# Upper halves of two layer norms made from the rows in front of the norm, in a fused transformer kernel

## The reference, cut to what matters

```
x = x + tanh(g_xattn[0]) * attention(layernorm(x), ctx)           # 8 heads, rotary, 128 context rows
x = x + tanh(g_ffn[0])   * ternary_ffn(layernorm(x))              # 512 -> 2048, relu^2, -> 512, low-rank part
x = x + tanh(g_xattn[1]) * (layernorm(x) @ W1.T + mean(ctx) @ W2.T + b)
x = x + tanh(g_ffn[1])   * bit_ffn(layernorm(x))                  # int8 activations, ternary weights, gelu

layernorm(x) = (x - mean(x)) / sqrt(var(x) + 1e-5)
```

## Time and profile before

| what | value |
|---|---|
| time, three runs | 1179.39, 1174.64, 1177.76 us; median 1177.76 |
| profiled execution, span | 1176.7 us (the page lists no other time for it) |
| TensorE busy | 1094.3 us, 93% |
| VectorE busy | 953.5 us, 81% |
| ScalarE busy | 799.4 us, 68% |
| GpSimd busy | 591.5 us, 50% |
| mean granted TensorE clock | 0.978 of full speed |

### The profile page before, as it was taken

How to read it: one execution, slowest core, us unless ns; L and a number is a source line. 1 busy time by engine, 2 the same in 40 slices (tenths; PEclk the granted TensorE clock), 3 DMA queues, 4 the chain that set the end, 5 groups by cost and what they waited for, 6 DMA issues and landing times.

```text
span 1176.7 us, 22172 instructions
## 1 busy us (share of the span) xinstructions
PE 1094.3 (93%) x8270; PEld 677.4 (58%) x8558; DVE 953.5 (81%) x1989; ACT 799.4 (68%) x1575; POOL 591.5 (50%) x567
## 2 busy tenths in 40 slices
PE   5776699999999999999899999999999999999997
PEld 5544456474655656475655656475656656564654
DVE  4796868778789888788878798898879886998667
ACT  3988947676683958576584857676674957586545
POOL 4243545464653746454544656555545555564431
PEclk9888799999999999999999999999999999999999
DMA  9959651434525343533625252443436242432210
GB/s 339 367 153 309 204 122 47 99 81 77 126 59 117 69 116 73 104 81 68 126 53 136 57 123 68 89 110 77 108 55 145 45 119 61 103 69 55 68 45 27
DMA packets 273802, 128.11 MB, mean 109 GB/s; under 512 B 247568, under 2 KB 248080, under 8 KB 272016
## 3 DMA queue, kind: packets, MB, share of 16 engines
q1 hardware_dynamic: 273136, 125.73, 41.8%
q10 hardware_dynamic: 560, 0.96, 0.3%
HBM read 57.19 MB, written 8.39 MB: 56 GB/s over the span
## 4 chain that ended last, share of the span: by engine, by line
PE 55%; ACT 17%; DVE 16%; POOL 5%; issue 4%; DMA 2%; SPq 0%; ACTq 0%; DVEq 0%
PE ps L1861 14%; PE ps L1835 10%; PE ps L1904 6%; PE ps L1920 5%; PE ps L1788 5%; ACT e L966 4%; PE ps L1735 4%; PE ps L1883 4%; ACT rl L1002 3%; ACT hid L1007 2%; ACT sq L1013 2%; PE ps L1760 1%; DVE st L1369 1%; PE ps L1841 1%; PE ps L1775 1%
## 5 line engine op out<-in xcount | busy, mean ns | idle before, releaser
L1835 PE MATMUL ps<-xT,fcT 128*128 128x256 f16 x2048 | 262.5, 276 | 10.8 <-ACT rl L1002 7.1
L749 POOL TENSOR_TENSOR rs<-ve,nhalf 128x1 f32<-128x1 f32 x160 | 101.7, 638 | 306.1 <-DVE ve L1374 222.8
L1861 PE MATMUL ps<-pjT,hid 128*128 128x512 fp8e4 x1024 | 232.3, 379 | 2.6 <-POOL hid L776 1.6
L1835 PEld LDWEIGHTS ps<-xT,fcT 128*128 128x128 fp8e4 x2048 | 200.1, 99 | 52.6 <-ACT rl L1002 10.0
L776 POOL TENSOR_TENSOR hid<-sq,hid 128x512 f16<-128x512 f32 x128 | 163.1, 1279 | 80.3 <-ACT sq L1013 79.4
L1861 PEld LDWEIGHTS ps<-pjT,hid 128*128 128x128 f16 x1024 | 98.0, 98 | 98.3
L1002 ACT ACTIVATE rl<-ps,rsf 128x256 f32<-128x256 f32 x256 | 106.4, 469 | 25.0 <-PE ps L1841 24.8
L966 ACT ACTIVATE e<-ps,nmb,sig 128x128 f32<-128x128 f32 x256 | 113.1, 462 | 7.2 <-DVE nmb L1412 6.9
L1904 PE MATMUL ps<-w1T,q4T 128*128 128x512 fp8e4 x480 | 114.2, 379 | 0.7 <-issue 0.6
L1058 ACT ACTIVATE q<-h 128x2048 f16<-128x2048 f32 x30 | 57.3, 1910 | 79.3 <-DVE h L1531 79.3
L781 POOL TENSOR_TENSOR e<-e,einv 128x512 f32<-128x512 f32 x64 | 70.1, 1100 | 78.5 <-DVE einv L1416 78.5
(11 more groups left out here) (243 smaller groups left out, 2025.7 us busy)
## 6 DMA issues: line engine op xcount, KB each, us to landing
xb<-in_x SPq DMA_DIRECT2D x16, 512.0 KB, 3.6
xa<-in_x SPq DMA_DIRECT2D x15, 512.0 KB, 4.0
out<-r SPq DMA_DIRECT2D x30, 256.0 KB, 2.3
rope<-in_rope SPq DMA_DIRECT2D x16, 384.0 KB, 3.2
h<-in_w1T SPq DMA_DIRECT2D x6, 1024.0 KB, 5.8
h<-in_w2T SPq DMA_DIRECT2D x6, 1024.0 KB, 6.4
h<-in_wkvT SPq DMA_DIRECT2D x2, 1024.0 KB, 12.6
hid<-in_w_fc SPq DMA_DIRECT2D x2, 1024.0 KB, 9.9
```

The lines of the kernel that those rows point to most:

```text
L1835: pe.matmul(ps[:, FFN0 + m % 2, a * G:(a + 1) * G], fcT[:, k, f * P:(f + 1) * P], xT2[:, xs, k, :], start=(xs == 0 and k == 0), stop=False)
L1861: mm = pe.matmul(ps[:, FFN0 + t, :], hid[:, xs, c, t * P:(t + 1) * P], pjT[:, c, :], start=(c == 0 and xs == 0), stop=(c == FC - 1 and xs ...
```

## The change

ScalarE no longer copies the normed rows. It computes the upper half itself from the rows in front of the norm, as rows * rs + shift, with rs and shift as columns (one number per row). VectorE makes the shift = -mean * rs, a new 128x1 operation (ln_shift), directly in front of ln_apply. The normed rows are still made by VectorE, for the lower half. The waits change with it: ScalarE waits for the shift instead of the normed rows; GpSimd's lower halves wait for both the upper half and the normed rows; add_cb, which overwrites r2, waits for the upper half as well. Two semaphores of the setup (c_rsf, c_sc) are folded into others, which makes room for the new ones. The tables of the order are the same.

```diff
+        shift = sb("shift", [P, 2, TILES], F32)
...
             def x2_lo(g, t):
                 need(pool, x2hi, TILES, g, t)
+                need(pool, xn2_done, TILES, g, t)
                 rest(x16f[:, t, 1, :], xn2[:, t, :], x16f[:, t, 0, :], x2lo)
...
                 need(pool, x3hi, TILES, g, t)
+                need(pool, xn3, TILES, g, t)
                 rest(x16b[:, t, 1, :], x3n_of(g)[:, t, :], x16b[:, t, 0, :], x3lo)
...
                 need(pool, xn3, TILES, g, t)
+                if not final(g):
+                    need(pool, x3hi, TILES, g, t)
                 pool.tensor_tensor(r2_of(g)[:, t, :], r2_of(g)[:, t, :], cb[:, g // PER_BATCH, :], ALU.add).then_inc(x2c, 1)
...
             def x2_hi(g, t):
                 need_dma(act, xT2_in[t], g - 1)
-                need(act, xn2_done, TILES, g, t)
-                act.activation(x16f[:, t, 0, :], xn2[:, t, :], ACT.Copy).then_inc(x2hi, 1)
+                need(act, shift2, TILES, g, t)
+                act.activation(x16f[:, t, 0, :], r1[:, g % 2, t, :], ACT.Identity, bias=shift[:, 0, t:t + 1],
+                               scale=rs[:, 1, t:t + 1]).then_inc(x2hi, 1)
...
                 need_dma(act, q4T_in[t], g - 1)
-                need(act, xn3, TILES, g, t)
-                act.activation(x16b[:, t, 0, :], x3n_of(g)[:, t, :], ACT.Copy).then_inc(x3hi, 1)
+                need(act, shift3, TILES, g, t)
+                act.activation(x16b[:, t, 0, :], r2_of(g)[:, t, :], ACT.Identity, bias=shift[:, 1, t:t + 1],
+                               scale=rs[:, 2, t:t + 1]).then_inc(x3hi, 1)
...
+            def ln_shift(rsem, done, g, n, t):
+                need(dve, rsem, TILES, g, t)
+                dve.tensor_scalar(shift[:, n - 1, t:t + 1], mv[:, n, t, 0:1], rs[:, n, t:t + 1], -1.0, ALU.mult, ALU.mult)\
+                    .then_inc(done, 1)
...
             def ln2_apply(g, t):
+                ln_shift(rs2, shift2, g, 1, t)
                 if t == 0:
                     need(dve, sq_done, FC // 2, g - 1, FC // 2 - 1)
                 ln_apply(rs2, xn2_done, g, 1, t, r1[:, g % 2, t, :], xn2[:, t, :])
...
             def ln3_apply(g, t):
+                if not final(g):
+                    ln_shift(rs3, shift3, g, 2, t)
                 ln_apply(rs3, xn3, g, 2, t, r2_of(g)[:, t, :], x3n_of(g)[:, t, :])
```

More of the change, by code:

```diff
@@ L259, in build @@
          c_vhi, c_vlo, c_cs, c_csb, c_cps, c_cb, c_tanh, c_wchain, c_scale, c_b2, c_rows, c_thr, c_rowd, c_quant, c_quantg,
-         c_tern, c_quantp, c_lowps, c_low, c_lowzero, c_lowF, c_lowt, c_lowact, c_bnd, c_rsf, c_scd,
-         c_scps, c_sc, c_asum, c_asumps, c_mean, c_round, c_lift, c_clip) = [sem(n) for n in (
+         c_tern, c_quantp, c_lowps, c_low, c_lowzero, c_lowF, c_lowt, c_lowact, c_bnd, c_scd,
+         c_scps, c_asum, c_asumps, c_mean, c_round, c_lift, c_clip) = [sem(n) for n in (
             "d_ctx d_wv d_kr d_wq d_wo d_wx d_wc d_small d_rows d_u d_b1 c_const c_kps c_vps c_kru c_krot "
@@ L264, in build @@
             "c_vhi c_vlo c_cs c_csb c_cps c_cb c_tanh c_wchain c_scale c_b2 c_rows c_thr c_rowd c_quant c_quantg c_tern c_quantp "
-            "c_lowps c_low c_lowzero c_lowF c_lowt c_lowact c_bnd c_rsf c_scd c_scps c_sc c_asum "
+            "c_lowps c_low c_lowzero c_lowF c_lowt c_lowact c_bnd c_scd c_scps c_asum "
             "c_asumps c_mean c_round c_lift c_clip").split()]
@@ L279, in build @@
         (ln1, rs1, xn1, x1hi, x1lo, q_ps, rot_mul, rot_sum, q_hi, q_lo, s_ps, s_max, s_bias, s_exp, s_inv,
-         s_norm, p_hi, p_lo, pv_ps, ao_hi, ao_lo, wo_ps, x1_done, ln2, rs2, xn2_done, x2hi, x2lo, low_ps,
+         s_norm, p_hi, p_lo, pv_ps, ao_hi, ao_lo, wo_ps, x1_done, ln2, rs2, shift2, xn2_done, x2hi, x2lo, low_ps,
          part_ps, part_b, low_b, low_r, low_done) = [sem(n) for n in (
              "ln1 rs1 xn1 x1hi x1lo q_ps rot_mul rot_sum q_hi q_lo s_ps s_max s_bias s_exp s_inv "
-             "s_norm p_hi p_lo pv_ps ao_hi ao_lo wo_ps x1_done ln2 rs2 xn2_done x2hi x2lo low_ps "
+             "s_norm p_hi p_lo pv_ps ao_hi ao_lo wo_ps x1_done ln2 rs2 shift2 xn2_done x2hi x2lo low_ps "
              "part_ps part_b low_b low_r low_done").split()]
@@ L287, in build @@
             "up_ps relu sq_done hid_hi hid_lo down_ps down_mul x2_done").split()]
-        (ln3, rs3, xn3, x3hi, x3lo, x2c, wx_ps, x3_done, ln4, rs4, z4, q4_done, x3b, w1_ps,
+        (ln3, rs3, shift3, xn3, x3hi, x3lo, x2c, wx_ps, x3_done, ln4, rs4, z4, q4_done, x3b, w1_ps,
          h_done, gelu, sqsum, z5, rs5, q5_round, q5_done, w2_ps, out_done) = [sem(n) for n in (
-             "ln3 rs3 xn3 x3hi x3lo x2c wx_ps x3_done ln4 rs4 z4 q4_done x3b w1_ps "
+             "ln3 rs3 shift3 xn3 x3hi x3lo x2c wx_ps x3_done ln4 rs4 z4 q4_done x3b w1_ps "
              "h_done gelu sqsum z5 rs5 q5_round q5_done w2_ps out_done").split()]
@@ L996, in up_act @@
                 if first(g) and m == 0:
-                    act.wait_ge(c_rsf, 1)
+                    act.wait_ge(c_bnd, 7)
                     for place in (0, 1):
@@ L1245, in hidden_scale @@
                 dve.wait_ge(c_bnd, 6)
-                dve.tensor_scalar(rsf[:, :], scf[:, :], rho[:, :], None, ALU.mult).then_inc(c_rsf, 1)
+                dve.tensor_scalar(rsf[:, :], scf[:, :], rho[:, :], None, ALU.mult).then_inc(c_bnd, 1)
             def mix_row():
@@ L1352, in prepare @@
                     dve.wait_ge(d_rows, 32)
-                    dve.tensor_scalar(scbc[:, :], ps[:, 0, :], c1[:, :], None, ALU.mult).then_inc(c_sc, 1)
+                    dve.tensor_scalar(scbc[:, :], ps[:, 0, :], c1[:, :], None, ALU.mult).then_inc(c_scd, 1)
                     dve.tensor_scalar(b2bc[:, :], b2bc[:, :], tg[:, 3:4], None, ALU.mult).then_inc(c_b2, 1)
@@ L1456, in x2_out @@
                 if first(g) and t == 0:
-                    dve.wait_ge(c_sc, 1)
+                    dve.wait_ge(c_scd, 3)
                 need(dve, down_ps, TILES, g, t)
@@ L1815, in up @@
                     pe.wait_ge(c_quantp, 16)
-                    pe.wait_ge(c_sc, 1)
+                    pe.wait_ge(c_scd, 3)
                 if m == 0:
```

## The result

The changed kernel takes 1188.65 us in the median of four runs (1187.17 to 1193.33), the kernel before 1178.58 us in the runs beside it. The two medians are 10.1 us apart; the ratio on record, which isn't that of the medians, is 1.0108 with a 95% interval of 1.0087 to 1.013: slower by 12.7 us of 1177, at least by 10. The forecast was 1185.2 us and 7.4 us of loss. One later run of the kernel before took 1911 us at a mean clock of 0.56; it is left out of the ratios.

A forecast was written before the change was run, and what follows sets the result against it. TensorE, busy 97% of the steady stretch, was taken as the bound, its short waits leading to other engines. Terms 3.0 + 2.5 + 2.1 - 0.2 + 0 = 7.4 us gave 1185.2 us against the runs' median, range 1175 to 1197.

The forecast's parts named there:

- the main step: GpSimd's addition after the third norm must wait for ScalarE's upper half, about 24 us later in all, which delays TensorE.
- the term of the wait: Cost to TensorE of GpSimd's late additions: 3.0 us at three followed places plus 2.5 us for the rest.
- the three places: Late additions at 1077.96, 572.98 and 768.11 us, followed to TensorE: 1.3, 0.9 and 0.8 us lost.
- The remaining places: The other 16.1 us of later additions on GpSimd, put at 2.5 us, with ends of 0.8 and 6.1.
- most are short and have gaps behind them: Reason given for pricing the other 16.1 us of GpSimd's new waits at only 2.5 us.
- VectorE's 2.1 us: 62 new 128x1 shifts at 214 ns, 13.3 us of work, of which the chain's 16% counts: 2.1 us.
- The upper end of 13.3 us: Highest cost of VectorE's 62 shifts, if all their work counted; the other end was 0.
- ScalarE at 0: 62 longer activations add 11.5 us of work, but 36 end earlier and 26 later; put at 0.
- Second norm -0.2: Its upper half ends 0.15 us earlier where ScalarE waited: a gain of 0.2 us, ends 0 and -1.0.
- Same by cover: Rival: the late additions are covered because much of TensorE's input was ready before; 1180 us, chance 0.24.
- Faster by ScalarE's earlier start: Rival: ScalarE's upper halves start earlier and shorten TensorE's waits, down to 1171 us; chance 0.12.
- Much slower by collisions: Rival: late GpSimd additions meet VectorE work and stretch it, 14 us in all, 1192 us; chance 0.18.

The follow-up runs named there:

- e4: Kernel before with only the added wait of GpSimd's addition for ScalarE's upper half of the third norm: 1189.64 us, ratio 1.0093.
- e3: Changed kernel with GpSimd's addition writing to the second norm's dead input rows, so without the wait for ScalarE: 1180.27 us, ratio 1.0022.
- e1: Changed kernel with the second norm put back as before, only the third norm changed: 1187.75 us, ratio 1.0089.
- e6: e3 with the addition's wait for ScalarE put back for tile 1 of each group, 15 of 30 additions: 1185.02 us, ratio 1.0079.
- e5: e3 with the addition's wait for ScalarE put back for tile 0 of each group, 15 of 30 additions: 1185.28 us, ratio 1.0075.
- e8: Kernel before with the 62 VectorE shifts added but read by nobody, and the setup's two semaphores folded: 1179.97 us, ratio 1.0034.
- e7: e3 with the second norm put back as before, leaving 30 shifts and 30 longer activations: 1176.59 us, ratio 1.0009.
- e2: Changed kernel with the third norm and the addition's wait put back as before, only the second norm changed: 1182.08 us, ratio 1.0033.
- e10: e9 with the third norm changed as well, its upper half made from the rows in front of the norm: 1184.79 us, ratio 1.0067.
- e9: Kernel before with GpSimd's addition writing to other rows and not waiting for the third norm, except in the last group: 1184.45 us, ratio 1.0068.
- e12: Changed kernel with rotation sums put in front of the second tile's addition on GpSimd in the fifth and tenth group: 1191.38 us, ratio 1.0126.
- e11: Kernel before with ScalarE's 62 upper halves in the longer two-column form; the new column also moved buffers by 32 bytes: 1184.41 us, ratio 1.0074.

## Why the prediction came out as it did

**Right: the main step.** The added wait of GpSimd's addition is the cause. It alone costs 10.9 us (e4, 8.0 to 13.8), and taking it away gives back 10.1 (the changed kernel's +12.7 less e3's +2.6; 8.4 by their medians). Its marks came as written: idle time before the addition over 45 us (59.8), released by ScalarE; scores over 7.5 us (10.7); mix of the 15th group over 1.5 us (2.02); TensorE's idle time after 180 us up by more than 4 us (10.1).

**Mis-sized: the term of the wait.** 3.0 + 2.5 = 5.5 us were put there, 8 to 11 were measured. Of the three places two were right: 1.1 us near 1088 for 1.3, 0.7 near 580 for 0.9. The third, 768 us, was put at 0.8 and cost 3.1: the first 1.6 as the upper end of the prediction had it (0 to 1.5), the rest by a fall of TensorE's clock, which no term had and which e1, e4 and e6 don't have at this place, after waits of 2.02 to 2.22 us (they lose 1.4 to 1.6 us there). The remaining places were put at 2.5 us, 16% of 16.1; they lost 4.5 (9.4 less these three). The additions came about as late as computed (22.5 to 26 us for 24), so the size that failed is the price of a late one, and the step is "most are short and have gaps behind them": e5 and e6 show that 15 waits of either tile are enough for 6 to 7 us, so the loss isn't the affair of a few places. Whether the two halves simply add up isn't shown: they stand 6.2 + 6.7 = 12.9 us above e3, for 10.1 with both, a difference that the intervals, 1.4 to 2.6 us to either side, cover.

**The other terms.** VectorE's 2.1 us: e8 has 4.0 (2.6 to 5.5), which lies above it, and e7 with half of the shifts and of the longer activations 1.1 (-0.2 to 2.4), which agrees with it; the place isn't known. The upper end of 13.3 us was no end: a shift takes up 0.12 us of VectorE's queue and not 0.21, 7.8 us in all. ScalarE at 0: no run shows it alone, e7 holds it under 2.4 us for 30 of the 62. The 0.15 us by which an upper half ends earlier came out: at 21 of the third norm's 30 tiles it ends 0.27 us earlier behind the norm's start, which the shift puts 0.12 us later. Second norm -0.2: the sign was wrong, e2 has +3.9, of which its 32 shifts are a part that no run separates; its trace shows 2.1 us at one transfer (last section), which no row of before shows. That the whole came out 3.5 us above the forecast's 1185.2 and inside its range is in part the width of the range: the main term alone was short by 3 to 5 us.

**The rivals.** "Same by cover" fails by e4. "Faster by ScalarE's earlier start" fails by e2, and by e7 and e10, which are not under their counterparts; a gain of a microsecond that the shifts take back isn't excluded. "Much slower by collisions": VectorE's busy time rose by 5.6 us, far from the 14 that were its mark. But the mechanism exists: the longest of the third norm's rows goes from 1.38 to 1.59 us, and e9, which brings GpSimd's addition beside the norm on purpose, stretches it by 6.4 us in all. Here the Trainium skill, "SBUF — State Buffer", section "SBUF: two separate sides", holds that a VectorE instruction in a mode that uses two ports, or with two inputs in SBUF, and a GpSimd instruction exclude each other, and that the second one waits for the other's whole instruction. The trace agrees for the norm's 128x512, in e9 (1.48 us for 0.54, ending 0.28 us behind the addition) as in the kernel before (1.38 us, ending 0.28 us behind a lower half on GpSimd); in which mode it runs no row says. The prediction left the condition out when it asked whether a shift would wait as well. It didn't: seven of the 62 shifts start while GpSimd is in the middle of a 128x512 instruction, and they take 203 to 208 ns.

No kernel here beats the one before. e7 comes nearest, with no difference that can be measured.

## What to carry to other kernels

When a reader of a buffer moves to another engine, look first at who overwrites the buffer: the new wait lands on the writer's queue and is paid by everything behind it, here with some 10 us for additions that start 0.5 us later in the median of 30 tiles. Give the writer another buffer (rows that are dead by then cost no memory) rather than a wait. And don't take idle time in front of an instruction for slack to be removed: in an order written out by hand it may be what keeps two engines off each other; test it by taking the wait away, not by arguing. And before a place in the trace is given a price, look at the clock of both executions: a fall in one of them is as large as many a step.

## What the runs showed of the hardware

**A fall of the clock at a short wait.** From 178 to 1155 us, where TensorE is otherwise at 1.00, the 14 kernels' executions have 15 falls to 0.50, of 3.4 us each. Each stands at a wait of TensorE of 1.94 to 3.06 us, mostly behind it (780 us, rows above), in two cases from within it. Such a fall costs up to 1.7 us on top of the wait: 1.5 us at 780 us, 1.6 at 1091 us in e5. The length of the wait doesn't tell whether it comes: 17 other waits of 1.91 to 2.89 us had none, among them 2.89 us at 588 us in e1 and 2.02 us at 1098.63 us in the changed kernel. At 182 us, behind a wait of 2.2 us, the clock fell in the changed kernel and in e3, where the step is 3.3 and 3.4 us, and not in e2, e5, e6 and e12, where it is 2.1 or 2.2. What decides is open.

**Two packets behind an instruction packet.** In the changed kernel, e2, e3, e5, e6 and e12, which all have the second norm changed, the same transfer (second group, second tile, issued near 180 us) lands 4.2 to 4.4 us after its issue; in the kernel before and e1, e4, e7 to e10, which have not, 2.7 or 2.8 (3.0 in e11). Queues in the changed kernel, packets, MB and share, for the microseconds from 180 and from 181:

```profile
q8 instruction: 1, 0.02, 6.3%
q1 hardware_dynamic: 42, 0.01, 3.8%
...
q1 hardware_dynamic: 2, 0.00, 0.3%
```

All but two of the transfer's packets are through when one packet of 0.02 MB of instructions is moved, and the last two follow a microsecond later. TensorE waits for it with no releaser named:

```profile
177.86 1.23 SPq L651 DMA_TRANSPOSE xT<-x16f  x1
...
182.18 0.40 PE L1816 MATMUL ps<-xT,vcol 128*32 128x256 f16 x8 [2.17 <-issue]
```

All 14 traces have such an instruction packet of 16 KB here, of 0.9 to 1.7 us, and its place in time goes with the delay. In the six kernels with the delay it starts 0.04 to 0.17 us before the last of the transfer's other packets, and the two late ones, of 4 bytes each, come within 0.02 us of its end. In the eight without, it starts 0.03 us before the transfer's last packet at the earliest, and up to 0.5 us behind it. That it holds the two back fits all 14, and no run moved it alone; what ties its place to the second norm's change isn't known.

**Thirty-two bytes.** Buffers moved by 32 bytes, off the multiples of 64, made most turning transfers 0.3 to 0.6 us longer (e11, rows above) and raised the transfer queue's share of the engines from 35.8 to 39.8% between 180 and 1176 us. One direction of one move was tried. The Trainium skill, "DMA: Bandwidth & Descriptors", section "DMA Transpose (X-bar)", asks for 32-byte alignment in SBUF; both programs keep it, and the transfers at the moved places were the slower ones, except those of the quantized rows, which took 2.4 us for 2.3.

**ScalarE's columns.** 808 and 809 ns against 621 and 626 are 187 and 183 ns for two columns. The Trainium skill, "ScalarE: Activation LUTs", section "What ACT_TABLE_LOAD costs", gives about 93 ns for each; the trace agrees.
